# Flamingo-style gated cross-attention, two layers: how the 65 keys left after twelve whole chunks are scored, exponentiated and weighed

## The reference, cut to what matters

```python
q = (x @ Wq + bq).reshape(B, N, 16, 16)        # N = 2048 tokens, layer-normed in layer 0
k = (y @ Wk + bk).reshape(B, M, 16, 16)        # M = 1601 keys
v = (y @ Wv + bv).reshape(B, M, 16, 16)
attn = softmax(einsum('bnhd,bmhd->bhnm', q, k) / 4, axis=-1)
out = einsum('bhnm,bmhd->bnhd', attn, v)       # then output projection (layer 1: a ReLU MLP)
```

## Time and profile before

| | |
|---|---|
| median of 3 runs | 1462.54 us (1461.04 to 1464.5) |
| profiled execution, span of its instructions | 1461.2 us (its own time is not listed apart from the span) |
| TensorE matmul busy / weight load busy | 1340.8 us (92%) / 707.4 us (48%) |
| ScalarE busy | 985.1 us (67%) |
| VectorE busy | 591.4 us (40%) |
| attention, layer 0 / layer 1 | 65.8 to 468.5 us / 765.3 to 1200.8 us |

### The profile page before, as it was taken

The page is one execution under the profiler, slowest core; times in us unless marked ns, Lnnn a source line. Parts: engine busy times, 40 slices in busy tenths (PEclk is TensorE's granted clock), DMA queues, the critical chain, the costliest instruction groups (busy, mean ns, idle before and its releaser), DMA issues. The chain is left out here.

```text
span 1461.2 us, 31936 instructions
## 1 busy us (share of the span) xinstructions
PE 1340.8 (92%) x13180; PEld 707.4 (48%) x13180; DVE 591.4 (40%) x1253; ACT 985.1 (67%) x1186; POOL 174.4 (12%) x188
## 2 busy tenths in 40 slices
PE   7799999999999998999769999999999986399994
PEld 4333333333333655999633334334334325299983
DVE  7412143152332354434451123562662664544435
ACT  4599999999998233322359995995995980155532
POOL 2000000000000331233200000000000000166540
PEclk9999999999999999999979999999999996599998
DMA  7671010100100914211438010110111115022214
GB/s 209 164 124 28 20 27 21 27 20 20 27 24 21 308 58 141 79 52 45 110 109 175 20 29 13 35 28 16 34 28 48 66 35 169 18 66 73 70 59 173
DMA packets 66268, 101.88 MB, mean 70 GB/s; under 512 B 10218, under 2 KB 48366, under 8 KB 65224
## 3 DMA queue, kind: packets, MB, share of 16 engines
q1 hardware_dynamic: 60168, 83.52, 21.0%
q0 software_dynamic: 5952, 16.26, 3.4%
HBM read 69.04 MB, written 26.21 MB: 65 GB/s over the span
## 5 line engine op out<-in xcount | busy, mean ns | idle before, releaser
L1317 ACT ACTIVATE arena<-ps 128x1024 f32<-128x1024 f32 x556 | 565.5, 1306 | 52.8 <-PE ps L1057 52.8
L1057 PE MATMUL ps<-arena 99*32 99x512 bf16 x6656 | 467.7, 384 | 17.2 <-PEq L867 10.9
L1057 PEld LDWEIGHTS ps<-arena 99*32 99x32 bf16 x6656 | 148.1, 95 | 419.5 <-issue 165.5
L1317 ACT ACTIVATE wqkv<-ps 128x1024 f32<-128x1024 f32 x276 | 306.3, 1306 | 20.6 <-PE ps L1057 20.6
L1073 PE MATMUL ps<-arena 128*32 128x512 f32 x2224 | 288.7, 593 | 0.8 <-ACT arena L1317 0.8
L1413 DVE COPY work<-ps 128x512 f32<-128x512 f32 x30 | 20.7, 691 | 346.3 <-PE ps L1073 346.3
L1899 PE MATMUL ps<-work,arena 128*128 128x128 f32 x1184 | 147.7, 281 | 2.7 <-DVE work L1991 1.6
L1899 PEld LDWEIGHTS ps<-work,arena 128*128 128x128 f32 x1184 | 146.5, 197 | 7.0 <-DVE work L1991 4.0
L1073 PE MATMUL ps<-wqkv,arena 128*32 128x512 f32 x1104 | 143.5, 593 | 0.0
L991 POOL DMA_INDIRECT work<-xn_img,fetch x62 | 60.3, 972 | 585.3 <-DVEq L1037 540.7
L1913 PE MATMUL ps<-arena,work 128*128 x496 | 117.2, 380 | 0.0
(11 more groups left out here) (219 smaller groups left out, 1198.2 us busy)
## 6 DMA issues: line engine op xcount, KB each, us to landing
arena<-in_ew SPq DMA_DIRECT2D x16, 512.0 KB, 5.7
arena<-q_img SPq DMA_DIRECT2D x32, 192.0 KB
arena<-y_tok SPq DMA_DIRECT2D x12, 512.0 KB, 6.7
arena<-k_img SPq DMA_DIRECT2D x8, 624.0 KB, 13.7
q_img<-work SPq DMA_DIRECT2D x18, 256.0 KB, 2.7
k_img<-work SPq DMA_DIRECT2D x21, 208.0 KB, 2.4
arena<-q_img SPq DMA_DIRECT2D x32, 128.0 KB
arena<-in_rg SPq DMA_DIRECT2D x8, 512.0 KB, 7.8
```

The costliest lines, as they stand in the source:

```text
L1057: last = nc.tensor.matmul(ps[i * VW:(i + 1) * VW, buf + j, :], k2[0:ROWS + SHIFT, h, at:at + VW], q2[0:ROWS + SHIFT, h, :], start=True, st ...
L1317: nc.scalar.activation(probs[(b * STEPS + u) % RING], ps[:, buf:buf + 2, :], ACT.Exp, scale=SCALE).then_inc(s_exp, 1)
```

## The change

The last chunk of scores now holds 64 whole keys of two heads, one head in rows 0 to 63 and one in rows 64 to 127, so that the four heads of a group need one unit and not two. Key 1600 is left over: its score is made by four matmuls whose weights are that key's column repeated 32 times (one bank, 128 x 512), ScalarE exponentiates this half-size unit into `last_exp` (in the rows of `xn` that are free then), and VectorE, when it empties the sums, adds `last_exp` times the value of key 1600 (`last_v`, one scalar per row; 1 in the row that sums) with one scalar_tensor_tensor in place of the copy. The values of the last chunk are therefore projected three times (rows 0 to 63, rows 64 to 127, and the row of key 1600), zeroed where the other head's keys stand, and key 1600's values go through DRAM into the partitions where VectorE needs them.

```diff
 def project_v(c, bank):
+    else:
+        keys = slice(c * P, c * P + HALF)
+        pieces = [(ps[0:HALF, bank, 0:D], keys), (ps[HALF:P, bank, 0:D], keys),
+                  (ps[0:1, bank, D:2 * D], slice(M - 1, M))]
...
 def sync(sp):                                    # end of layer 0's preparation
+    if l == 0:
+        sp.wait_ge(s_va, NC)
+        store_last_row(sp, 0)                     # 1 DMA; load_last_values: 4 DMAs after k2 of group 1
...
 def scores(b, w):
+    if c == NC - 1 and half:                      # key 1600 of four heads: 4 matmuls
+        tiles = [(0, j, HG * g + j, k2[0:ROWS + SHIFT, HG * g + j, M - 1:M]
+                  .broadcast_to([ROWS + SHIFT, VW])) for j in range(HG)]
+    elif c == NC - 1:                             # 64 keys of two heads per bank: 8 matmuls
+        heads = [(j, i, HG * g + 2 * j + i // 2, c * P + i % 2 * VW)
+                 for j in range(2) for i in range(4)]
...
 def _(act):
+    if k == READ:                                 # k = 25, last unit of a group
+        if b * NG + g >= 2:
+            act.wait_ge(s_u, b * NG + g - 1)
+        nc.scalar.activation(last_exp[:, g % 2, :], ps[:, buf, :], ACT.Exp, scale=SCALE
+                             ).then_inc(s_exp, 1)
+        continue
...
 def group(b, g):
-    nc.vector.tensor_copy(pv_sb, ps[:, 6 + g % 2, :]).then_inc(s_copy, 1)
-    nc.vector.stream_shuffle(out=sums, in_=ps[:, 6 + g % 2, :], mask=[DH] * VW).then_inc(s_u, 1)
+    nc.vector.scalar_tensor_tensor(out=pv_sb, in0=last_exp[:, g % 2, :], scalar=last_v[:, g:g + 1],
+                                   in1=ps[:, 6 + g % 2, :], op0=ALU.mult, op1=ALU.add
+                                   ).then_inc(s_u, 1)
+    nc.vector.stream_shuffle(out=sums, in_=pv_sb, mask=[DH] * VW).then_inc(s_copy, 1)
...
 def last_group():
-    nc.vector.stream_shuffle(out=sums, in_=ps[:, 6 + g % 2, :], mask=[DH] * VW).then_inc(s_copy, 1)
+    nc.vector.scalar_tensor_tensor(out=pv_sb, in0=last_exp[:, g % 2, :], scalar=last_v[:, g:g + 1],
+                                   in1=ps[:, 6 + g % 2, :], op0=ALU.mult, op1=ALU.add
+                                   ).then_inc(s_u, 1)
+    nc.vector.stream_shuffle(out=sums, in_=pv_sb, mask=[DH] * VW).then_inc(s_copy, 1)
```

More of the change, by code:

```diff
@@ L56 @@
 MW = (M - 1) // 4 + 1
+HALF = P // 2
+UNITS = 2 * NC
+READ = UNITS - 1
 SAFE = 40.0
@@ L115, in build @@
         top2 = sb("top2", [P, 2])
+        sum_row, last_v = sb("sum_row", [P, 1]), sb("last_v", [P, NG])
         eb1 = sb("eb1", [P, E, 4])
@@ L194, in build @@
         hidT, at = view(work, at, [4, QB])
+        last_row = work[0:1, at:at + D]
         y_tmp, at = view(work, at, [2 * D])
+        last_exp = xn[:, (NB - 1) * TB:NT, :].rearrange("p t d -> p (t d)").rearrange("p (g q) -> p g q", q=QB)
         G = KD * F
@@ L331, in build @@
         s_kones = keep("key_ones_set")
+        s_lrow, s_lv = keep("last_row_stored"), keep("last_values_in")
         def load_wk(eng, l):
@@ L395, in pad_v @@
             chain(nc.gpsimd.memset(v_aug[:, 0:NC - 1, :, DH:DH + 1], 1.0))
-            chain(nc.gpsimd.memset(v_aug[0:M - (NC - 1) * P, NC - 1, :, DH:DH + 1], 1.0))
+            for i in range(2):
+                own, other = slice(i * HALF, (i + 1) * HALF), slice((1 - i) * HALF, (2 - i) * HALF)
+                chain(nc.gpsimd.memset(v_aug[own, NC - 1, i::2, DH:DH + 1], 1.0))
+                chain(nc.gpsimd.memset(v_aug[other, NC - 1, i::2, 0:DH], 0.0))
         def ones_row(pool, n=1):
@@ L1052, in scores @@
                                 pe.wait_ge(s_exp, b * STEPS + last_read + 1)
[L1053 to L1059, removed]
+                            if c == NC - 1 and half:
[4 more added lines that the diff above has]
+                                         for j in range(2) for i in range(4)]
+                                tiles = [(j, i, h, k2[0:ROWS + SHIFT, h, at:at + VW]) for j, i, h, at in heads]
+                            else:
+                                heads = [(j, i, HG * g + 2 * half + j, c * P + i * VW)
+                                         for j in range(2) for i in range(4)]
+                                tiles = [(j, i, h, k2[0:ROWS + SHIFT, h, at:at + VW]) for j, i, h, at in heads]
+                            for j, i, h, keys in tiles:
+                                last = nc.tensor.matmul(ps[i * VW:(i + 1) * VW, buf + j, :], keys,
+                                                        q2[0:ROWS + SHIFT, h, :],
+                                                        start=True, stop=True, skip_group_check=True)
                             last.then_inc(s_qk, 1)
@@ L1314, in _ @@
                             act.wait_ge(s_qk, b * STEPS + u + 1)
-                            if half == 0 and b * NG * NC + w >= RING // 2:
-                                act.wait_ge(s_pv, b * NG * NC + w - RING // 2 + 1)
-                            nc.scalar.activation(probs[(b * STEPS + u) % RING], ps[:, buf:buf + 2, :],
+                            if k == READ:
[4 more added lines that the diff above has]
+                                continue
+                            n = in_ring(b, u)
+                            if n >= RING and weighed_of(n - RING) + 1 > freed:
+                                freed = weighed_of(n - RING) + 1
+                                act.wait_ge(s_pv, freed)
+                            nc.scalar.activation(probs[n % RING], ps[:, buf:buf + 2, :],
                                                  ACT.Exp, scale=SCALE).then_inc(s_exp, 1)
```

57 lines of the change are left out of this document (48 added, 9 removed).

## The result

The changed kernel takes 1447.54 us (median of 4 runs, 1445.73 to 1449.38), the kernel before beside it 1461.79 (4 runs, 1459.44 to 1464.5): ratio 0.9898, interval 0.9876 to 0.992. The profiled execution took 1448.27 us, with a span of 1446.4 against 1461.2: 14.8 us less.

A forecast was written before the change was run, and what follows sets the result against it. ScalarE was taken to set the pace outside the tails, TensorE inside them. Attention -12.4, preparation +1.9 and layer 1's last group +0.8 sum to -9.7 us: 1462.5 becomes 1452.8 us, range 1449.5 to 1459.5.

The forecast's parts named there:

- TensorE is the bound: Rival for attention: every group saves only TensorE's 0.22 us, -4.3 us in all, giving 1458.2 us; chance 0.12.
- Attention, 12.4 us: Both layers' attention: 26 groups save 0.427 us of ScalarE, six ending in tails save 0.22 of TensorE; 12.4 us less.
- Repeated-column weights: Score matmuls of key 1600: loading one column read 32 times might be slow and stall TensorE once a group; counted at nothing.
- VectorE's weighing: Emptying the sums in each group: a scalar_tensor_tensor of 0.752 us replaces the copy; VectorE has room, so at nothing.
- the new ScalarE wait: Before each half-size unit ScalarE waits for the emptying of the group two before, over 23 us old; at nothing.
- the four DMAs: Loads of `last_v` in SyncE's queue ahead of group 2's loads, 2.5 us plus the store's wait; hidden.
- layer 1's values: Projected at the end of layer 0: 1.72 us more of TensorE and two copies, with 3 us of cover; at nothing.
- No change: Rival: slow repeated-column loads eat the gain, needing about 0.30 us a group beyond its 1.4 us of room; 1462.5, chance 0.08.
- The last group of layer 1, +0.8: End of layer 1's attention: weighing before the shuffle, with nothing else running, adds 0.8 us, at least 0.7.
- End of layer 0's preparation, +1.9: Three pieces for the last value chunk delay the path to the first scores by 1.9 us, between 1.3 and 2.5.
- the sum: Whole kernel: -12.4 + 1.9 + 0.8 = -9.7 us, bounds 1450.8 and 1458.8 us; chance 0.74.
- The clock: Rival, slower: TensorE's low clock at attention's start lasts more steps, six eating the gain, a whole group giving 1474; chance 0.04.

The follow-up runs named there:

- act_twice: Changed kernel with each half-size exponential made twice, undoing ScalarE's saving: 1461.75 us, ratio 0.9992 to the kernel before.
- pe_twice: Changed kernel with the four score matmuls of each key-1600 unit issued twice, undoing TensorE's saving: 1456.76 us, ratio 0.996 to the kernel before.
- after_again: Changed kernel, unchanged, run again for five more rounds: 1446.48 us, ratio 0.9891 to the kernel before.
- before_5424: Kernel before with 56 fewer matmuls in layer 1's never-taken branch, so its attention begins at TensorE call 5424: 1459.38 us, ratio 0.9984.
- before_pad: Kernel before with 4 and 196 more matmuls in the never-taken branches of layers 0 and 1: 1464.46 us, ratio 1.0016.
- prep_only: Kernel before with only the change's preparation (three value pieces, copies, store, loads) and the old attention: 1465.41 us, ratio 1.0018.
- after_pad: Changed kernel with 56 more matmuls in layer 1's never-taken branch: 1453.0 us, ratio 0.993 to the kernel before.

## Why the prediction was wrong

- **What bounds the kernel: right.** ScalarE outside the tails, TensorE inside, shown by act_twice and pe_twice in their rows. The rival "TensorE is the bound" is refuted: matmuls were "busy" 99.7% of layer 0's stage in pe_twice, and its plain groups were no longer.
- **Attention, 12.4 us: the mechanism right, the total partly by luck.** 12.0 by the traces, standstills set aside. The spacing of 0.49 for the half-size exponential was 0.48; only the duration, said to be 0.6, had a median of 0.87. Plain groups fell from 23.83 to 23.41 (0.43 forecast: 0.42). That a group is worth 0.43 outside the tails and 0.22 inside did not hold at a block's end: the fourth group fell from 24.64 to 23.92, the tail group from 27.64 to 27.54 and the one behind it from 23.24 to 23.14, 0.92 together for 1.07. The last group of each layer, with 0.75 for 0.43, made up for most of it.
- **Repeated-column weights, VectorE's weighing, the new ScalarE wait, the four DMAs, layer 1's values: at nothing, right.** (In "No change" the room for slow loads is overstated: TensorE's 12 x 1.73 + 1.51 = 22.3 us against ScalarE's 12 x 1.83 + 1.41 = 23.4 leave 1.1 us of a group and not 1.4. Nothing hangs on it: doubled, the four matmuls cost 0.21.) The last group of layer 1, +0.8: 0.79.
- **End of layer 0's preparation, +1.9: too much, in two ways.** The three pieces cost 1.0 us and not 1.72. And I took the distance from there to the first scores ("All engines meet here and scores begin at 65.84, so this is on the path") as a fixed 7.2 us. It isn't: with the change's preparation it was 4.2 us in 8 of 10 profiles and 7.6 or 7.7 in two; with the old one 6.8 to 7.2 in all five. Which of the two comes goes with when an instruction transfer starts. Of the earlier start after_again loses 1.4 us again, in its standstills of 0.39 and 1.04 us; pe_twice, as early and without them, loses nothing.
- **The step that failed** is the sum itself: it adds up the work that is executed, and holds the rest of the kernel as it was. "The bounds of the sum are 1462.5 - 13.7 + 2.0 = 1450.8" had no term for standstills that the kernel before has at one place of its code and not at another. The diff made layer 1's attention begin 56 calls earlier in TensorE's code, and 2.34 + 0.84 us of standing still, most of it next to a late transfer of instructions, went with it: two thirds of the 4.5 us missed. With them the time would have been 1450.7, inside the range. before_5424 shows 2.3 us of this by itself (0.16%, interval 0.05 to 0.28%). The rest is argued from the profiles, since most executions have none: the cheaper preparation gives 0.9, the shorter gap in layer 0 up to 3 where it occurs, and against them stand new standstills of 0.85 to 1.4 us in layer 0.
- **The clock** as rival, slower: not seen. Both stages were granted 0.99 and 1.00. At the start of layer 0 the lower level lasted longer in the profiled execution (0.53 from 68 to 72 us, 0.81 in the kernel before), and there the first group saved nothing; after_again was granted 0.87 in those 4 us.

Open: what makes the transfer in layer 0 start early or late in one and the same program, and why the changed preparation mostly gets it early; four more calls in TensorE's never-taken branch of layer 0 did not bring it (before_pad, 6.75 us), and the other engines' code was not tried. Also the tails of block 2: their standstill ends 1.8 us behind a transfer in the kernel before (both profiles), but 3.1 us behind one in prep_only, where the tail is longest (42.31 us). Also what the unprofiled executions of pe_twice (all three, 5 to 6 us above the profiled one) and after_pad (four of five, 3 to 5 us) spend their time on.

## What to carry to other kernels

Before summing terms, look in the trace for standstills of the bounding engine in which it waited for nothing, above all behind jumps: if a transfer of the instruction queue ends 1 to 2 us before they do, they belong to the layout of the code, and an edit ahead of them can remove or add 2 to 3 us. A kernel whose never-executed branch is padded by a few dozen instructions shows how large this is, and two such paddings give a first idea of the error bar that a comparison of two versions really has. Where an engine's pace is in question, double one engine's share of the edit at a time and read the spacing of a periodic event (here the shuffles), not the median and not the busy share.

## What was not expected of the hardware

- Never-executed matmuls in TensorE's stream moved the time by 3 to 6 us (after_pad); 56 fewer made the kernel before 0.16% faster.
- TensorE's instructions came in transfers of 16 KiB, one per 256 of them; where one came late, matmuls went on 1.3 to 2.1 us behind its end, after losses of up to 3.4 us.
- A jump on a value that all engines read, with the meeting behind it, cost 8.8 us for two places: by the rows 5.1 us (7.22 to 2.10) at the first and 1.5 + 2.3 (wait and standstill) at the second.
- One program had 4.18 and 7.61 us at the same jump in two executions, with the instruction transfer before the jump in one and behind it in the other.
- A 128x512 exponential in the stream lasts 0.87 us in the median and sets the next one back by 0.48 only.
